# A decoder layer on one core: queries and keys split into high and low float32r parts for the logits, turned outputs moved to the accumulators' bank

## What is computed

```python
def _cope(q, sim, pos_emb):
    G = jax.nn.sigmoid(sim)
    P = jnp.flip(jnp.cumsum(jnp.flip(G, axis=-1), axis=-1), axis=-1)
    P = jnp.minimum(P, T_MAX - 1)
    P_floor = jnp.floor(P)
    ...
    E = jnp.einsum('bnc,ct->bnt', q, pos_emb)
    ...
    return w * E_ceil + (1.0 - w) * E_floor
...
q, k, v = (to_heads(q), to_heads(k), to_heads(v))
sim = jnp.einsum('bid,bjd->bij', q, k) * scale
sim = sim + _cope(q, sim, pos_emb)
attn = jax.nn.softmax(sim, axis=-1)
out = jnp.einsum('bij,bjd->bid', attn, v)
...
return out @ Wout + b_out
```

## Time and profile before

| | |
|---|---|
| runs before, median of 3 | 2649.62 us (2647.76 to 2652.51) |
| the profiled execution, its own time | 2652.94 us |
| its span, first to last instruction | 2651.1 us |
| granted TensorE clock, mean | 0.985 of 2.4 GHz |
| TensorE, VectorE, ScalarE, GpSimd busy | 93%, 76%, 61%, 7% |
| transfers, mean | 28 GB/s, 10% of the 16 engines' time |

### The profile page before, as it was taken

One profiled execution on the slowest core, in us unless ns is written; L12 is line 12 of the kernel. 1 busy time (PEld: TensorE's weight loads), 2 busy tenths in 40 slices (PEclk: granted clock), 3 DMA queues, 4 the chain that ended last, 5 costly groups with the idle time before them and its releaser, 6 DMA issues. The chain is left out here.

```text
span 2651.1 us, 64197 instructions
## 1 busy us (share of the span) xinstructions
PE 2472.1 (93%) x18687; PEld 1691.1 (64%) x18687; DVE 2006.4 (76%) x5179; ACT 1615.9 (61%) x3383; POOL 190.4 (7%) x289
## 2 busy tenths in 40 slices
PE   7999998999899989998999999999999988999997
PEld 5666665666566656666666566666666656777776
DVE  6888888888888888888888888888899960232322
ACT  4666666666666666666666666666666663444442
POOL 0000000000000000000000000000000000111111
PEclk9999999999999999999999999999999998999998
DMA  2010101010101010100101110101001002100100
GB/s 68 20 33 20 34 20 32 20 34 20 32 20 34 20 32 21 32 21 21 29 24 29 25 29 24 29 24 29 22 21 40 21 17 68 34 26 34 36 26 6
DMA packets 96567, 74.74 MB, mean 28 GB/s; under 512 B 24590, under 2 KB 92303, under 8 KB 96464
## 3 DMA queue, kind: packets, MB, share of 16 engines
q1 hardware_dynamic: 96464, 73.15, 10.1%
HBM read 14.26 MB, written 2.10 MB: 6 GB/s over the span
## 5 line engine op out<-in xcount | busy, mean ns | idle before, releaser
L748 DVE TENSOR_REDUCE mx<-Sc 128x1 f32<-128x1024 f32 x512 | 621.5, 1214 | 160.2 <-PE Sc L544 159.7
L552 PE MATMUL ring<-ident,probs 128*128 128x128 f32 x4096 | 620.9, 284 | 115.2 <-ACT attn L418 65.3
L409 ACT ACTIVATE probsT<-ring 128x512 f32<-128x512 f32 x1024 | 584.7, 596 | 132.1 <-PE ring L552 129.2
L552 PEld LDWEIGHTS ring<-ident,probs 128*128 128x128 f32 x4096 | 446.3, 145 | 258.3 <-ACT attn L418 127.0
L430 ACT ACTIVATE probs<-Sc,nbias 128x1024 f32<-128x1024 f32 x512 | 565.6, 1117 | 4.7 <-DVE nbias L765 4.7
L544 PE MATMUL Sc<-qk,q_now 64*128 64x512 f32 x2048 | 539.4, 637 | 22.4 <-issue 16.0
L566 PE MATMUL out<-probsT,V_now 128*64 128x128 f32 x8192 | 530.0, 277 | 0.0
L566 PEld LDWEIGHTS out<-probsT,V_now 128*64 128x64 f32 x8192 | 439.5, 137 | 76.3 <-ACT probsT L409 57.9
L712 DVE COPY_PREDICATED z<-mask,z 128x224 f32<-128x224 int16 (+5 forms) x768 | 389.7, 507 | 34.4
L418 ACT ACTIVATE attn<-ring,rsum 128x64 f32 (+1 forms) x256 | 80.3, 314 | 436.5 <-PE ring L575 420.7
L544 PEld LDWEIGHTS Sc<-qk,q_now 64*128 64x128 f32 x2048 | 173.6, 188 | 217.8 <-issue 217.8
(11 more groups left out here) (116 smaller groups left out, 2301.8 us busy)
## 6 DMA issues: line engine op xcount, KB each, us to landing
q_now<-qk SPq DMA_DIRECT2D x256, 64.0 KB, 2.0
xv<-xT SPq DMA_DIRECT2D x113, 128.0 KB, 2.2
q_far<-qk SPq DMA_DIRECT2D x128, 64.0 KB, 1.9
V_now<-V SPq DMA_DIRECT2D x16, 512.0 KB, 3.2
at<-attn SPq DMA_DIRECT2D x16, 512.0 KB, 3.2
probs<-in_x_dram SPq DMA_DIRECT2D x4, 512.0 KB, 5.3
wqk<-in_L_attn_Wq_dram SPq DMA_DIRECT2D x32, 64.0 KB, 2.1
xin<-in_x_dram SPq DMA_DIRECT2D x16, 128.0 KB, 2.8
```

The costliest lines, as they stand in the source:

```text
L409: nc.scalar.activation(probsT[:, u, 4 * s:4 * s + 4, :], ring[k % 2][:, :].rearrange("p (t q) -> p t q", q=P), ACT.Copy).then_inc(slot_out, 1)
L552: last = nc.tensor.transpose(ring[k % 2][:, j * P:(j + 1) * P], probs[:, u, (4 * s + j) * P:(4 * s + j + 1) * P], ident[:, :])
L748: nc.vector.tensor_reduce(mx[:, u, half:half + 1], Sc[:, half * HALF:(half + 1) * HALF], AX.X, ALU.max).then_inc(dve_unit, 1)
```

## The change

The logits and the window are computed from a high and a low part of queries and keys, both of type float32r. ScalarE writes the projection twice, as `full` (float32) and rounded as `hi`; GpSimd subtracts (`remainder`) and writes `lo`. SyncE moves the four quarters of `hi` and `lo` (`move`) to `q2` and `kk`, where partitions 0 to 63 hold high and 64 to 127 low parts. A product takes 128 rows: the high queries twice, one upon the other, against the high and low keys, then the low queries twice, added in the same bank. `full`, `hi` and `lo` have one buffer each. The turned output goes to columns 128 to 191 of the bank `out` instead of a ring slot, so two slots fewer are used per body, the scaling gets semaphores of its own (`turned`, `scaled`), and the next outputs wait for `scaled`. On TensorE the last two banks of logits alternate with groups of transposes. The heads have one layout now, so bodies no longer differ by parity, and V's tiles are read in plain order.

```diff
-SLOTS0 = 8 + 2 * PAIRS - 6
-SLOTS = 12
-LATE_SLOTS = 10
+SLOTS0 = 8 + 2 * PAIRS - 4
+SLOTS = 10
+LATE_SLOTS = 8
+TURN = P
...
-    def __init__(self, first=False, proj=True):
-        self.turn0 = 0
-        self.last = [1, 2, 3, 4]
-        at = 6 if first else 5
-        self.qk, self.values = at, at + 1
-        at += 2 if proj else 0
-        self.turn1 = at
-        at += 0 if first else 1
+    def __init__(self, proj=True):
+        self.last = [0, 1, 2, 3]
+        self.qk, self.values = 4, 5
+        at = 6 if proj else 4
         self.now = [at, at + 1, at + 2, at + 3]
-
-
-def token_tile(ct):
-
-    bank, i = ct // 4, ct % 4
-    return 2 * (bank // 2 * 4 + bank % 2 + i // 2 * 2) + i % 2
...
-        wqk = sb("wqk", [P, DC, 3 * C])
+        wqk = sb("wqk", [P, DC, 2 * C])
         wv = sb("wv", [P, DC, 2 * C])
-        qk = sb("qk", [P, 2, 2, QK])
-        qk_scale = sb("qk_scale", [P, 2])
+        kk = sb("kk", [P, 2, NTAB], F32R)
+        q2 = sb("q2", [P, 2, N], F32R)
+        full = sb("full", [P, STEP])
+        hi = sb("hi", [P, STEP], F32R)
+        lo = sb("lo", [P, STEP], F32R)
+        qk_scale = sb("qk_scale", [P, 1])
...
+            def load_queries(dst, g, landed):
+
                 h, t = g // PAIRS, g % PAIRS
-                sp.dma_start(q_far[C:P, :], queries(h, odd, t)).then_inc(far_in, 16)
-
-            def load_now(g, odd):
-                h, t = g // PAIRS, g % PAIRS
-                sp.dma_start(q_now[0:C, :], queries(h, odd, t)).then_inc(now_in, 16)
-                sp.dma_start(q_now[C:P, :], queries(h, odd, t)).then_inc(now_in, 16)
+                at = bass.ds(t * STEP, STEP)
+                for part in range(2):
+                    src = q2[part * C:(part + 1) * C, h % 2, at].bitcast(F32)
+                    for half in range(2):
+                        sp.dma_start(dst[half * C:(half + 1) * C, part, :].bitcast(F32), src).then_inc(landed, 16)
+
+            def load_far(g):
+                load_queries(q_far, g, far_in)
+
+            def load_now(g):
+                load_queries(q_now, g, now_in)
+
+            def move(s):
+
+                h, b = s // PAIRS, (s + 7) % PAIRS
+                at = bass.ds(b * STEP, STEP)
+                for part, src in enumerate((hi, lo)):
+                    rows = slice(part * C, (part + 1) * C)
+                    sp.dma_start(q2[rows, h % 2, at].bitcast(F32), src[0:C, :].bitcast(F32)).then_inc(moved, 16)
+                    sp.dma_start(kk[rows, h % 2, at].bitcast(F32), src[C:P, :].bitcast(F32)).then_inc(moved, 16)
...
+            for s in range(PAIRS):
+                sp.wait_ge(lo_done, s + 1)
+                move(s)
+                if s == 1:
+                    sp.wait_ge(moved, 2 * 64)
+                    load_far(0)
+                    load_now(0)
+                if s == 4:
+                    sp.wait_ge(moved, 5 * 64)
+                    sp.wait_ge(near_full, 1)
+                    load_far(1)
...
+                if far:
+
+                    wait_apart(sp, near_full, g + 2, waited)
+                    wait_apart(sp, moved, (G if late else g + 4) * 64, waited)
+                    load_far(g + 2)
                 if head:
 
                     wait_apart(sp, out_full, g * 2, waited)
                     load_values(g)
-                if far:
-
-                    wait_apart(sp, near_full, g + 2, waited)
-                    wait_apart(sp, slot_out, 8 + 2 * PAIRS if first else base - 4, waited)
-                    load_far(g + 2, odd)
                 if tile:
-                    wait_apart(sp, slot_full, base + Slots(first).values + 1, waited)
+                    wait_apart(sp, slot_full, base + Slots().values + 1, waited)
                     load_tile(g + 1)
+                if not late:
+                    wait_apart(sp, lo_done, g + (PAIRS + 1), waited)
+                    move(g + PAIRS)
                 wait_apart(sp, bank_full, g * 4 + 4, waited)
-                load_now(g + 1, not odd)
-
-            body(0, False, first=True)
-            body(1, True)
-            with sp.Fori(2, PAIRS, 2) as g:
-                body(g, False)
-                body(g + 1, True)
+                load_now(g + 1)
...
+            def remainder(s):
+
+                pool.wait_ge(hi_done, s + 1)
+                if not (isinstance(s, int) and s == 0):
+                    pool.wait_ge(moved, s * 64)
+                nc.gpsimd.tensor_tensor(lo[:, :], full[:, :], hi[:, :].bitcast(F32),
+                                        ALU.subtract).then_inc(lo_done, 1)
+
+            def slope_product(c):
                 pool.wait_ge(shifted, c * CH + CH)
                 nc.gpsimd.tensor_tensor(prod[:, :, 1:W], frac[:, :, 1:W], z[:, 1, :, 1:W],
                                         ALU.mult).then_inc(prod_done, 1)
 
-            with pool.Fori(0, G) as c:
-                body(c)
+            for s in range(PAIRS):
+                remainder(s)
+            slope_product(0)
+            with pool.Fori(0, LASTP) as g:
+                remainder(g + PAIRS)
+                slope_product(g + 1)
...
-                nc.scalar.activation(qk[:, h % 2, int(odd), bass.ds(b // 2 * STEP, STEP)], ring[k % 2][:, 0:STEP],
-                                     ACT.Copy, scale=qk_scale[:, int(odd):int(odd) + 1])\
+                if not (isinstance(s, int) and s == 0):
+                    act.wait_ge(lo_done, s)
+                    wait_apart(act, moved, s * 64, waited)
+                nc.scalar.activation(full[:, :], ring[k % 2][:, 0:STEP], ACT.Copy, scale=qk_scale[:, :])\
                     .then_inc(slot_out, 2 if alone else 1)
+                nc.scalar.activation(hi[:, :], ring[k % 2][:, 0:STEP], ACT.Copy, scale=qk_scale[:, :]).then_inc(hi_done, 1)
...
-            def scale(g, u, base, k):
+            def scale(g, u):
 
                 h, t = g // PAIRS, g % PAIRS
                 act.wait_ge(rsum_done, g * 2 + u + 1)
-                wait_apart(act, slot_full, base + k + 1, waited)
-                nc.scalar.activation(attn[:, t * 2 + u, bass.ds(h * C, C)], ring[k % 2][:, 0:C], ACT.Copy,
-                                     scale=rsum[:, u:u + 1]).then_inc(slot_out, 1)
+                wait_apart(act, turned, g * 2 + u + 1, waited)
+                nc.scalar.activation(attn[:, t * 2 + u, bass.ds(h * C, C)], out[:, TURN:TURN + C], ACT.Copy,
+                                     scale=rsum[:, u:u + 1]).then_inc(scaled, 1)
...
                     empty_halves(g - 1, 0)
-                    scale(g - 1, 0, base, at.turn0)
-                    transposed(1, base, at.last)
+                    transposed(1, base, at.last, range(3))
+                    scale(g - 1, 0)
+                    transposed(1, base, at.last, range(3, 4))
...
-                pe.wait_ge(far_in, c * 16 + 16)
+                pe.wait_ge(far_in, c * 64 + 64)
                 for i in range(2):
-                    last = nc.tensor.matmul(near[:, i * (W + T):(i + 1) * (W + T)], q_far[C:P, i * P:(i + 1) * P],
-                                            qk[C:P, par, 1, HALF - W:QK], start=True, stop=True)
+                    for part in range(2):
+                        last = nc.tensor.matmul(near[:, i * (W + T):(i + 1) * (W + T)],
+                                                q_far[:, part, i * P:(i + 1) * P], kk[:, par, TAIL:NTAB],
+                                                start=part == 0, stop=part == 1)
...
-            def logits(par, u, half):
-
-                cols = slice(half * BANK, (half + 1) * BANK)
-                for r in range(2):
-                    rows = slice(r * C, (r + 1) * C)
-                    bank = half * 2 + r
-                    last = nc.tensor.matmul(Sc[:, bank * BANK:(bank + 1) * BANK], q_now[rows, u * P:(u + 1) * P],
-                                            qk[rows, par, r, cols], start=True, stop=True)
-                last.then_inc(bank_full, 1)
+            def logits(par, u, bank):
+
+                cols = slice(bank * BANK, (bank + 1) * BANK)
+                for part in range(2):
+                    last = nc.tensor.matmul(Sc[:, cols], q_now[:, part, u * P:(u + 1) * P], kk[:, par, cols],
+                                            start=part == 0, stop=part == 1)
+                if bank % 2:
+                    last.then_inc(bank_full, 1)
...
+                    if turned_before:
+                        wait_apart(pe, scaled, g * 2 + u, waited)
...
-            def turn(g, u, base, k):
+            def turn(g, u):
 
                 pe.wait_ge(halves_out, g * 2 + u + 1)
-                pe.wait_ge(slot_out, base + k - 1)
-                nc.tensor.matmul(ring[k % 2][:, 0:C], halves[:, u, :], fold[:, :],
-                                 start=True, stop=True).then_inc(slot_full, 1)
-
-            def body(g, odd, par, late=False, first=False, proj=True, val=True, far=True, far_par=None):
+                nc.tensor.matmul(out[:, TURN:TURN + C], halves[:, u, :], fold[:, :],
```

(39 more changed lines are left out.)

199 lines of the change are left out of this document (92 added, 107 removed).

## The result

The changed kernel takes 2981.08 us (median of 4 runs, 2979.38 to 2983.4), against 2649.62 for the kernel before: a ratio of 1.125, 95% interval 1.1228 to 1.1272. The kernel before has the median of its three fast runs here; a fourth, slow one took 3486.99 us and is left out. Slower, as forecast, but by 331 us instead of 68, and outside the range. The profiled execution took 2979.38 us, its span 2977.6.

A forecast was written before the change was run, and what follows sets the result against it. TensorE bounds the kernel now, VectorE close behind; afterwards two chains, at 16.9 us per body. Start +28, 110 bodies +33, eight without values +5, heads +3: +69 on 2652.9 gives 2722, 2718 against the median; range 2655 to 2790.

The forecast's parts named there:

- Chain B: From a body's first logits to its second tile's, 8.5 us, then through the parts and SyncE to q_now's landing, 8.2: 16.7 us.
- Chain A: Closed chain through VectorE, exponentials, halves, projection activation, hi_done and TensorE's transposes and banks back to VectorE: 16.6 us per body.
- TensorE's own work: TensorE's work per main-stage body after the change: about 16.3 us, down from 16.6.
- The start: Eight projection steps of 5.5 us, each waiting for the last one's moves; first logits at 61.6, +28 us.
- float32r, 0.213 per 512 columns: Logits products on TensorE: one pass of 512 columns at 2.4 GHz, 0.213 us; +0.2 us counted per body.
- Rival 3: float32r products take two or more passes: 19.7 us per body, near 3040 us in all; chance 0.05.
- The window: TensorE's window as four products of 240 columns: taken at today's 1.0 us, between 0.5 and 2.0.
- Rival 1: The window is dear, 2.0 us at float32's price: TensorE alone needs 17.3 us per body, total 2770; chance 0.22.
- The wait for hi: TensorE idle 0.6 to 0.7 us before the first query tile's transposes, released by the hi activation.
- The scaled wait: TensorE's outputs wait for the turn's scaling: 0.4 us lost per body.
- Rival 2: Alternating logits with transposes pays: both chains shorter than TensorE's work, bodies of 15.9 us, total 2601; chance 0.10.
- The last stage: The seven last bodies, at VectorE's floor of 15.33 us each: no change.

The follow-up runs named there:

- experiment 1: Changed kernel, with SyncE issuing the four q_now transfers before it waits for and moves the low part: 2738.35 us, ratio 1.0344.
- experiment 4: On experiment 1, singly: last-move wait only before the fourth bank, 2664.58 us; V projected before queries and keys, 2693.11; first turn and scaling one group earlier, 2702.0.
- experiment 2: Changed kernel with eleven extra unused products ahead of TensorE's wait for q_now in bodies with a projection: 2870.6 us, ratio 1.0843.
- 3, first edit: Kernel before the change, with q_now issued only after the window product of the same body: 2785.23 us, ratio 1.0526.
- Experiment 6: The four edits of experiment 5 plus a second buffer set for the eight starting steps and first q_far and q_now loads just ahead of moves: 2567.1 us, ratio 0.971.
- experiment 5, without the first edit: Changed kernel with the three edits of experiment 4 together, SyncE still issuing the moves ahead of q_now: 3058.79 us, ratio 1.1559.
- the four edits of experiment 5: Changed kernel with the edit of experiment 1 and the three of experiment 4 together: 2583.04 us, ratio 0.9764.
- experiment 3's second edit: Kernel before the change, with q_now issued only after the last outputs of the body: 3192.28 us, ratio 1.2053.

## Why the prediction was right or wrong

- **The bound and its signs: right.** Chain B, through `q_now`, decides; the idle time ahead of a body's first logits is released by a `q_now` transfer. One sign failed: for the second half of the second tile's logits VectorE waits 0.72 us in the full-clock body and 0.73 in the slow one, not over 1; the 1.48 us at 1114.82 are for the first tile, behind the half clock.
- **Chain A, 16.6 us: the length right, the links not all.** With `q_now` out of the way the bodies are 16.7 (experiment 1), and shortening the part through `hi_done` makes them 16.22 (experiment 4). But moving the turn, which is no link of the chain as I drew it, makes them 16.25 as well.
- **Chain B: the right path, its sum too small; this is the larger part of the miss.** The main stage was to cost 36 us and cost 278, of which 172 are the chain (experiment 2). From a body's first logits to its second tile's takes 8.25 us (1382.98 to 1391.23) where I had 8.5. The second half is 10.1 instead of 8.2: halves 0.12 and 0.32 (0.11 and 0.50 predicted), the two activations with their signal 1.01 (1.02), GpSimd 0.73 (0.73), and then three steps that I had too short. *Signal to SyncE*: in the body shown the low part starts at 1101.83 and takes 0.73 us; the first move is issued at 1103.02, 0.46 later, where I had 0.1. *Issue spacings*: three of 0.67 between the moves, one of 1.06 from the last move to `q_now`, three of 0.60 on average in `q_now`, 4.9 instead of 3.7; the 0.53 came from one pair of issues of one helper. *Landing and wake-up*: 2.6 instead of 2.06. Sum 18.3 instead of 16.7, seen in the full-clock body.
- **TensorE's own work: 15.4 us, not 16.3.** The full-clock body of 18.34 us has 2.93 of idle time ahead of its first logits; the rest, its other waits included, is 15.4. So the two errors add up: my sums left TensorE 16.7 - 16.3 = 0.4 us to wait for `q_now`, and the longer chain with the shorter work made 2.9 of it.
- **The step that failed outright: half clock was no term at all.** I noted 0.985 of the full clock and added up durations at that clock, though my own sum made TensorE wait for `q_now` in every body. After 2.9 us of idle time the products run at 1.2 GHz in most bodies and cost them 1.7 us more. The 106 us of experiment 2 are this term. At the 0.4 us of waiting that I had it might have stayed nothing: bodies with 1.0 to 1.3 us of it keep the full clock (experiments 1 and 3, first edit). The Trainium skill ("TensorE: Matmul & The Clock Gate", section "HAM oscillation — how this bites in real kernels") tells of a kernel whose waits for transfers between groups of products bring the clock down for each next group; the trace agrees that such waits do, with the granted 0.91 of a 20.02 us body against 1.00 of one with 18.34.
- **The start: +33 instead of +28.** A step takes 5.7 us instead of 5.5, by the same spacings, and the first logits start at 64.90 instead of 61.6. Experiment 6 confirms what the steps wait for.
- **float32r, 0.213 per 512 columns: right for the product, low for the group.** At the full clock four products take 1.20 us (1100.38) and eleven 2.74 (experiment 2), so (2.74 - 1.20)/7 = 0.22 for each further one. Rival 3 falls. The group of four was to take 1.02 and a pair 0.60; they take 1.20 and 0.72. What the Trainium skill ("FP8 and Floating Point Precision", section TensorE Precision Notes) states are four passes for true FP32 and the truncation to FP22 of the reduced form. That one pass is left was my own conclusion, which the 0.22 us bears out; the truncation no run here shows.
- **The window: cheaper than taken.** Four products of 240 columns take 0.69 us where I took 1.0. Rival 1 falls.
- **The wait for hi: half as long.** 0.36 us ahead of the first transposes (1101.94) instead of 0.6 to 0.7, and the profile names V's copy, the activation behind hi, as its end. Projecting V first takes it away.
- **The scaled wait: 0.72 instead of 0.4.** The profile names a copy (L430) as its end, but moving the turn and its scaling up brings it to 0.25. It stands on chain B too: where it is 0.24 us, the way from the first logits to the second tile's is 7.83 us instead of 8.25 (experiment 5, without the first edit). With `q_now` early it is worth 0.45 us a body.
- **Rival 2, the alternation pays: false for the change as it stands.** With the four edits of experiment 5 the bodies take 15.8 us, near this rival's 15.9, but VectorE is then busier than TensorE (1480 against 1425 of 1600 us), so it is not quite the rival's mechanism. I judged it by the change's own order alone.
- **The last stage: right in the main.** 15.31 us against 15.16. The 15.33 that I called VectorE's floor is no floor, since the changed kernel has bodies of 15.12.

## What to carry to other kernels

When a short transfer for the next step shares a queue with work that waits on another engine, put it ahead of that wait: here one exchange in SyncE's queue is worth 243 us. Price a new wait of TensorE's twice, once for its own length and once for what its products cost at half clock afterwards, if the row shows idle time near the 3 us of this case. And an edit that shortens another chain can lengthen the one that decides: the three of experiment 5 cost 78 us while `q_now` is late and gain 155 once it is early. Remove the deciding chain first and then judge them.

## What the hardware did that I had not expected

- The same 2.93 us of idle time was followed by half clock at 1401.33 and not at 1382.98, so the length of one wait alone does not decide it; what else does stays open. In the bodies read of experiment 1 a wait of 1.25 us didn't bring it about; the 2.87 and 3.24 us of experiment 3's second edit did.
- Issues in SyncE's queue have no one spacing: 0.53 before, here 0.60 on average within one helper's four, 0.64 to 0.71 between the moves, 1.06 from the last move to `q_now`.
- From the end of GpSimd's subtraction to SyncE's issue that waits for it 0.46 us pass (1102.56 to 1103.02), with the wait's own instructions in it.
